# A graph network's scatters on GpSimd, held back until TensorE has used up a set number of panels

## The reference, cut to what matters

```python
x = _layernorm(x + _L0_gnn_ref(x, edge_index, ...))   # three rounds of h + segment_sum(h[src], dst)
x = _layernorm(x + _L1_gnn_ref(x, edge_index, ...))   # mean over the edges
x = _layernorm(x + _L2_gnn_ref(x, edge_index, ...))   # mean over the edges
x = _layernorm(x + _L3_gnn_ref(x, edge_attr_128, src, dst, edge_weight, ...))
```

```python
w = edge_weight_raw / jnp.maximum(wsum, EPS)[dst]
msg = feat[src] * w[:, None]
neigh = jax.ops.segment_max(msg, dst, num_segments=N)
...
neigh2 = jax.ops.segment_sum(h[src] * w[:, None], dst, num_segments=N) / jnp.maximum(deg, 1.0)[:, None]
```

## Time and profile before

| | us |
|---|---|
| median of 3 runs (lowest to highest) | 4858.66 (4850.25 to 4870.81) |
| the profiled execution | 4872.96 |
| its span, from the first to the last instruction | 4871.1 |
| TensorE busy in the span | 3396.0 (70%) |
| GpSimd busy in the span | 1785.8 (37%) |
| first and last scatter start at | 946.0 and 2533.6 |

### The profile page before, as it was taken

How to read it: one execution, slowest core, us unless ns; L and a number is a source line. 1 busy time by engine, 2 the same in 40 slices (tenths; PEclk the granted TensorE clock), 3 DMA queues, 4 the chain that set the end, 5 groups by cost and what they waited for, 6 DMA issues and landing times.

```text
span 4871.1 us, 57973 instructions
## 1 busy us (share of the span) xinstructions
PE 3396.0 (70%) x22119; PEld 2919.8 (60%) x22119; DVE 2163.5 (44%) x4433; ACT 1955.0 (40%) x3073; POOL 1785.8 (37%) x1727
## 2 busy tenths in 40 slices
PE   4798888711113997995119999983577777777788
PEld 2676777610113996994019989973465565555666
DVE  8786777510003986884002233242233333333335
ACT  5687878610001444454006546552222222222221
POOL 3000000177772000887760000005665555555630
PEclk9999999855556998996559989996799888888999
DMA  4888888700003677442004424423355555555555
GB/s 152 224 231 238 230 224 232 218 14 4 7 7 77 219 240 251 133 130 37 4 7 150 135 67 149 130 60 108 93 198 187 197 188 182 181 195 196 187 193 180
DMA packets 299723, 712.84 MB, mean 146 GB/s; under 512 B 65270, under 2 KB 167445, under 8 KB 284214
## 3 DMA queue, kind: packets, MB, share of 16 engines
q1 hardware_dynamic: 167180, 436.77, 28.3%
q10 hardware_dynamic: 52298, 174.64, 10.2%
q0 software_dynamic: 79968, 97.68, 9.4%
HBM read 503.59 MB, written 254.50 MB: 156 GB/s over the span
## 4 chain that ended last, share of the span: by engine, by line
PE 47%; another core or an unknown queue 23%; ACT 9%; issue 7%; DVE 7%; DMA 5%; ACTq 1%; DVEq 0%; POOL 0%; SPq 0%; POOLq 0%
PE PS L740 21%; PE PS L1725 7%; DMA turned<-DEG 4%; PE PS L662 4%; PE PS L1711 3%; ACT CA L859 2%; ACT DEG L884 2%; PE PS L1701 2%; PE PS L625 2%; PE PS L1693 2%; PE PS L671 1%; DVE BB L1877 1%; PE PS L718 1%; ACT BB L1811 1%
## 5 line engine op out<-in xcount | busy, mean ns | idle before, releaser
L431 POOL DMA_INDIRECT PAN<-table,src_i x832 | 828.3, 996 | 1353.0 <-DMA table<-DEG 768.1
L972 POOL DMA_INDIRECT shares<-dst_f,spare x832 | 888.2, 1068 | 735.1 <-ACTq L777 427.2
L740 PE MATMUL PS<-CX,XH 125*128 125x376 f32 x2000 | 477.4, 318 | 260.0 <-issue 127.7
L740 PE MATMUL PS<-CX,XL 125*128 125x376 f32 x2000 | 472.7, 315 | 145.1 <-issue 145.1
L1819 ACT ACTIVATE BB<-PS 128x1024 f32<-128x1024 f32 x104 | 106.6, 1025 | 948.5 <-PE PS L1701 473.7
L740 PEld LDWEIGHTS PS<-CX,XH 125*128 125x128 f32 x2000 | 321.1, 197 | 276.8 <-issue 161.2
L740 PEld LDWEIGHTS PS<-CX,XL 125*128 125x128 f32 x2000 | 321.4, 197 | 145.0 <-issue 145.0
L537 ACT ACTIVATE CX<-PAN 125x3125 fp32r<-125x3125 uint8 x106 | 298.2, 2814 | 270.0 <-PE PS L740 233.2
L740 PE MATMUL PS<-CP,XH 125*128 125x376 f32 (+1 forms) x1330 | 313.3, 315 | 124.0 <-issue 79.4
L740 PE MATMUL PS<-CP,XL 125*128 125x376 f32 (+1 forms) x1330 | 309.8, 312 | 63.4 <-issue 63.4
L884 ACT ACTIVATE DEG<-PS 125x1250 uint8<-125x1250 bf16 x250 | 303.0, 1212 | 113.0 <-PE PS L671 61.8
(11 more groups left out here) (334 smaller groups left out, 7026.8 us busy)
## 6 DMA issues: line engine op xcount, KB each, us to landing
PAN<-counts SPq DMA_DIRECT2D x300, 390.6 KB
shares<-SSB ACTq DMA_DIRECT2D x70, 1600.0 KB
XP<-shares SPq DMA_DIRECT2D x50, 1600.0 KB
PAN<-shares SPq DMA_DIRECT2D x50, 1600.0 KB
BB<-start_penalty SPq DMA_DIRECT2D x104, 512.0 KB
shares<-blank ACTq DMA_DIRECT2D x15, 3200.0 KB, 13.9
turned<-DEG SPq DMA_DIRECT2D x50, 781.2 KB, 9.7
PAN<-turned SPq DMA_DIRECT2D x100, 390.6 KB
```

The source lines that it names most:

```text
L431: nc.gpsimd.indirect_dma_start(out=gbuf[g % 2][:, k, :], out_offset=None, in_=source, in_offset=bass.IndirectOffsetOnAxis(ap=src_i[:, t:t ...
L740: last = nc.tensor.matmul(wide_ps[b][h][:, 0:w], halves[part][0:TN, s * SUBJ + j, :], cast_part(v, j, h), start=(s == 0 and j == 0 and par ...
L972: nc.gpsimd.indirect_dma_start(out=shares_flat, out_offset=bass.IndirectOffsetOnAxis(ap=share_at[:, t:t + 1], axis=0), in_=share[:, t:t + ...
```

## The change

`pool_shares` gets one more wait ahead of every scatter, on `panel_used`. The function `share_pace` works out the count to wait for from `begun`, the scatter's number: scatters 0 to 207 go beside product 1, 208 to 415 beside product 2, 416 to 623 beside product 3 and the rest beside product 4. The k-th of a product's 208 waits until 10 + 90k/208 panels of that product are used, so the first waits for the end of chunk 0, and the last for panel 99. No instruction is added, and none moves on its own engine.

```diff
+        def share_pace(pool, begun):
+
+            half, i = divmod(begun, HL)
+            n, at = divmod(i, -(-HL // 2))
+            panels = NSUB + at * (NBLK - 1) * NSUB // -(-HL // 2)
+            pool.wait_ge(panel_used, NPAN + (1 + 2 * half + n) * NBLK * NSUB + panels)
+
...
                             pool.wait_ge(shares_out[begun % 3], 16 * (begun // 3))
+                        share_pace(pool, begun)
                         nc.gpsimd.indirect_dma_start(
```

## The result

The changed kernel took 4225.3 us in the median of four runs (4199.3 to 4246.9), the kernel before, beside it, 4860.5 (4850.3 to 4870.8). The ratio is 0.869, with a 95% interval from 0.863 to 0.875. The forecast was 4120, with a range from 4050 to 4250. The profiled run is the lowest of the four, 4199.3 us with a span of 4197.5, so its trace accounts for 673.6 of the 4871.1 us of before.

The account below looks back on a forecast made before the run. Some 770 us were taken to lie in two row stages slowed by GpSimd's scatters. 4873.0 - 509.4 - 252.6 + 23 = 4134.0 us, less 14 for the median, gave 4120 us, range 4050 to 4250.

Parts of the forecast that it names:

- Row stage of product 1: Rows ahead of product 1, with their loops: 593.6 us become 84.2 once scatters leave, saving 509.4.
- The twin: Row stage of product 2, same code as product 1's: 24.6 + 59.6 = 84.2 us, taken as measure, 15 us less allowed.
- Does GpSimd keep up?: Beside product 1, 189 of 208 scatters get out; 19 run into product 2's loops and rows, costing 23 us, at most 48.
- Row stage of product 3: Rows ahead of product 3: 362.6 us become 110, with 53 us beside late scatters; saves 252.6, from 238 to 267.
- the mode: In row stages beside scatters, TensorE's weight loads and matmuls start 1.40 us apart, each by itself, 70 us a panel.
- Products 3 and 4 with scatters: These products now carry 416 scatters: cost 0, as TensorE is full in both; upper bound 50 us each.
- DMA engines and the second wait: Panel loads sharing engines with scatters: 0, at most 12 us; the added wait per scatter: 0 to 0.1 us.
- Profiled run against median: Whole kernel: the median of runs lies 14 us below the profiled time, 4134 becoming 4120 us.
- The rival of the tails: Late scatters enter all four following stages and the mode is on at once: 4259 us, chance 0.11.
- The rival that scatters aren't the cause: Row stages of products 1 and 3 are slow by themselves; time stays at 4859 us, chance 0.03.
- The rival that product 3's stage keeps the mode for another reason: Product 1's stage loses the mode, product 3's keeps it after 2269: 4373 us, chance 0.03.
- The slower rival: TensorE enters chunk 1 in the mode, panels taking 56 us instead of 3.1; one whole product gives 8890 us, chance 0.03.

Follow-up runs that it names:

- Without tails: Changed kernel with only the first 125 scatters of product 1 and 160 of each other product issued, the rest left out: 4115.7 us, ratio 0.845.
- memsets in their place: Kernel before with each scatter replaced by four small memsets on GpSimd, each waited for, no DMA issued: 4099.0 us, ratio 0.841.
- one under way: Kernel before, unpaced, with each scatter waiting until the one just before has landed, in place of three under way: 5099.6 us, ratio 1.048.
- pauses: Kernel before, unpaced, with a pause of four small GpSimd memsets behind each scatter: 4882.8 us, ratio 1.001.
- the second half unpaced: Changed kernel with the pace for scatters 0 to 415 alone, 416 to 831 issued as fast as they go: 4636.1 us, ratio 0.953.
- the last comparison: Changed kernel run again unaltered beside the kernel before, on chip number 6: 3750.7 us against 3750.9, ratio 1.000.

## Why the forecast was right, and where it was off

The time, 4225 us, is in the range, 105 us above the forecast. In the traces the working came to 4134.0 and 4199.3 was measured, 65.3 more; the other 40 lie between profiled run and median.

1. **Row stage of product 1.** 505.9 us saved, 509.4 forecast. The twin was a good measure.
2. **Does GpSimd keep up?** It didn't, and by more than forecast. Product 1 let 138 out, not 189: its scatters came 2.2 us apart and not 1.61, most likely because of its blank stores, with which the DMA engines were at 0.70 (that wasn't tried apart; the trace has 31 waits for landings there, 60.9 us). But the tail cost 2.6 us rather than 23, and products 1 and 2 were 3.3 shorter. The 23 us had been read rightly as the price in product 1's own loops, which without scatters took 24.6 us too (939.7 to 964.3). What failed was to carry them over to the row stage of product 2, where the scatters came 2.1 us apart and not 1.3; this distance is the likely reason why that stage was spared.
3. **Row stage of product 3.** 148.3 us against 110, the first mis-sized term, 38.3 over. The failing step was "until there it is the stage of before", 53 us of normal progress, since the mode had begun late once. In the event the first stall began at once, while product 2's last transposes ended, and the tail was 85 us long in place of 53, because product 2 inherited product 1's scatters. Without tails the stretch from product to product is 55.8 us shorter, so the true floor was nearer to 93 than to 110, and the tail costs about 56.
4. **Products 3 and 4 with scatters.** The products cost 0.4 and 1.8 us, as forecast. What I took as nothing with an upper bound of 50 each were their tails, which came nearly as the bound's working had it (1.57 and 1.60 us per scatter, 36 and 33 of them late and not 40, tails of 48 and 43 us and not 62), and cost 18.8 + 27.0 = 45.8 us. This is the second mis-sized term. I had taken 0 "by TensorE's being full in both", which says nothing about the stages behind. Since products 3 and 4 give GpSimd no more room than product 2 did, the row for product 2 was the one to go by. The range had room for 50 us of this once, not twice; 45.8 fits in it.
5. **DMA engines and the second wait.** Neither shows: the chunks above take 30.95 and 30.00 us.
6. **Profiled run against median.** Taken as -14 and measured +26. The changed kernel's four runs spread over 47 us, the stalls being of varying length, and one profile can be at either end.

One reading of the rows was off without bearing on the sum: in rows 1 TensorE's two holes both stand at 1 tenth, in slices 9 to 12 and 20 to 21, and not at 1 and at 2 to 3.

The rival of the tails (4259 us) was in effect what happened in the row stages of products 3 and 4 and behind product 4, without its first term: of the 115 us that the tails cost by the medians, 37 were in the forecast (23, and 14 for the mode's rest). That it kept to single stalls was most likely due to their shortness; with 416 unpaced scatters from one stage on the full mode came back. The rival that scatters aren't the cause is out by four runs: memsets in their place, one under way, pauses, and the second half unpaced. The rival that product 3's stage keeps the mode for another reason falls by its 148.3 us. The slower rival, the mode inside the products, didn't come true in the changed kernel, whose chunks in products 3 and 4 took 30.0 to 31.6 us beside scatters. But its mechanism exists: with the second half unpaced TensorE entered chunk 1 of product 3 in the mode and needed 135.1 us for it. In the changed kernel the tails behind products 2 and 3 had ended 62 and 70 us ahead of the next chunk 1.

The Trainium skill, "DMA: Bandwidth & Descriptors", section "SWDGE vs HWDGE vs iDMA", says that DVE in its two-port mode locks GpSimd out of the memory that it writes its descriptors to. From this rule the prediction took that a scatter would need nearly 1.28 us beside products 3 and 4. The traces don't bear that out: 270.4/172 = 1.57 and 280.4/175 = 1.60 us with DVE busy 27% and 28% of the time, against 278.7/173 = 1.61 with DVE busy 85%. So DVE's busy share isn't what makes a scatter slow here; which of its operations run in that mode no trace here shows.

What no step had was the condition. I took the slow mode for a property of the program. It is one of the program on some chips, or on a chip in one condition, and in the other the same change saves nothing. Why, no run shows.

## What to carry to other kernels

If the chain has long pieces on an unknown queue and TensorE's instructions come one by one at a fixed distance, look for GpSimd issuing indirect DMAs back to back, and move them beside long runs of matmuls or space them; here 2.8 us apart cost nothing and 1.3 us apart cost most of a stage. If you move them, let them begin once TensorE is at full pace, since the mode, once on, carries over into the matmuls. Work that is paced by another engine needs its own rate in each place, taken from the nearest row, because what doesn't fit comes out in the stage behind, where it is dearest. And before a gain of that kind is counted, run the kernel before again on another chip: 635 us of gain were 0 when it took 3751 us itself.

## What the runs showed of the hardware that I had not expected

- The same kernel took 4860 to 4877 us in three comparisons and 3751 to 3761 in two, with nothing between them, and the four whose chip is known were on four chips (8 and 7 slow, 0 and 6 quick). A single indirect DMA takes GpSimd as long in both (gathers 944 ns, scatters 969); only the waits of others beside them differ.
- Such a stream beside panels, 1.6 us apart with TensorE busy 1.00 of the time, cost nothing in either condition. With TensorE slowed already it cost 105 us in one chunk.
- A direct DMA of 128 x 4 bytes from GpSimd is cheaper to issue than the indirect one, 0.54 against 0.97 us, but took 8.5 us to land with three under way, against the indirect one's 2.1 with one under way, so part of the 8.5 may be the wait behind the other two. SP's loads of 390.6 KB took 11.5 us beside them, against 3.4 with no scatters and 3.6 with indirect ones (the changed kernel in the last comparison).
